# Router work between the parts of the last output products, and logits in column halves

## The reference

```python
x = x + xattn(layernorm(x), ctx)      # 16 heads of 64: q, k, v, softmax(q k / 8) v, then w_o and b_o
x = x + ffn(layernorm(x))

# ffn, tokens flat: N = 4096, E = 8 experts
logits = x_flat @ router_w + router_b
gates = softmax(logits)
_, topk_idx = top_k(gates, 2)
expert_mask = one_hot(topk_idx, 8).sum(1)
pos = cumsum(expert_mask, axis=0) - 1              # place in the expert's buffer, over all tokens
expert_mask = expert_mask * (pos < 640)            # 640 = capacity
buf = zeros(8, 641, 256).at[e_idx, pos_c].add(dispatched)[:, :640]
h = gelu(buf @ w1 + b1)                            # 8 experts, hidden 1024
out = h @ w2 + b2
y = sum over experts of gathered out * (gates * valid)
```

## Time and profile before

| | us |
|---|---|
| median of 3 runs | 1019.17 |
| lowest, highest | 1018.17, 1020.28 |
| the profiled execution | 1018.17 |
| its span, first to last instruction | 1016.3 |
| TensorE busy | 979.9 (96%) |
| VectorE busy | 769.2 (76%) |
| ScalarE busy | 624.3 (61%) |
| GpSimd busy | 284.2 (28%) |

### The profile page before, as it was taken

One profiled execution on the slowest core, in us unless ns is written; L12 is line 12 of the kernel. 1 busy time (PEld: TensorE's weight loads), 2 busy tenths in 40 slices (PEclk: granted clock), 3 DMA queues, 4 the chain that ended last, 5 costly groups with the idle time before them and its releaser, 6 DMA issues.

```text
span 1016.3 us, 23196 instructions
## 1 busy us (share of the span) xinstructions
PE 979.9 (96%) x8382; PEld 883.9 (87%) x8382; DVE 769.2 (76%) x2088; ACT 624.3 (61%) x1736; POOL 284.2 (28%) x440
## 2 busy tenths in 40 slices
PE   7889999999999999999999999999888999999996
PEld 6778888888888888888888888888678999999996
DVE  6897768878787888878787887878755666776662
ACT  5777767777776777777676777777514333344330
POOL 5542021314223131313223131311442333222233
PEclk9999999999999999999999999999999999999998
DMA  8440101101010101101010110001105543444522
GB/s 241 144 114 2 33 2 33 43 13 55 14 40 15 33 13 33 44 2 43 12 32 6 33 35 6 17 5 50 58 18 178 137 96 80 113 128 129 136 26 26
DMA packets 48431, 56.74 MB, mean 56 GB/s; under 512 B 5324, under 2 KB 44218, under 8 KB 48192
## 3 DMA queue, kind: packets, MB, share of 16 engines
q1 hardware_dynamic: 39488, 46.30, 14.7%
q0 software_dynamic: 8832, 8.98, 5.5%
HBM read 36.01 MB, written 24.20 MB: 59 GB/s over the span
## 4 chain that ended last, share of the span: by engine, by line
PE 71%; DVE 18%; ACT 5%; issue 4%; DMA 0%; POOLq 0%; POOL 0%; another core or an unknown queue 0%; ACTq 0%
PE psum L561 29%; PE psum L756 11%; PE psum L658 8%; PE psum L644 7%; PE psum L628 7%; PE psum L672 7%; DVE prob L985 5%; ACT prob L819 3%; DVE negmax L974 3%; DVE kl L922 1%; DVE al L922 1%; PE psum L566 1%; DVE stats L929 1%; PE psum L719 1%; DVE ql L963 1%
## 5 line engine op out<-in xcount | busy, mean ns | idle before, releaser
L819 ACT ACTIVATE prob<-psum,negmax 128x256 f32<-128x256 f32 x512 | 239.1, 484 | 81.6 <-DVE negmax L974 81.6
L771 ACT ACTIVATE probt<-psum 128x512 f32<-128x512 f32 x256 | 157.6, 617 | 53.4 <-PE psum L644 51.1
L974 DVE TENSOR_REDUCE negmax<-psum 128x2 f32<-128x512 f32 x256 | 160.0, 683 | 22.0 <-PE psum L628 21.9
L985 DVE TENSOR_SCALAR prob<-prob,invtot 128x256 f32<-128x256 f32 x512 | 168.0, 392 | 4.5
L644 PE MATMUL psum<-ident,prob 128*128 128x128 f32 x1024 | 154.4, 275 | 3.3 <-DVE prob L985 1.7
L644 PEld LDWEIGHTS psum<-ident,prob 128*128 128x128 f32 x1024 | 120.5, 142 | 14.5 <-issue 4.4
L898 ACT ACTIVATE hid<-psum,b1t 128x640 f32<-128x640 f32 x64 | 50.9, 795 | 133.2 <-PE psum L561 133.2
L658 PE MATMUL psum<-probt,v 128*64 128x256 f32 x1024 | 124.6, 385 | 0.8 <-ACT probt L771 0.8
L541 POOL DMA_INDIRECT out_rows<-y,rowi x40 | 65.7, 1644 | 174.5 <-DVE y L1137 169.6
L505 POOL DMA_INDIRECT slot_table<-row,picki x64 | 64.7, 1011 | 170.2 <-DVE picki L1087 143.2
L819 ACT ACTIVATION_READ_ACCUMULATOR prob<-psum,negmax 128x1 f32 x512 | 111.2, 217 | 0.0
(11 more groups left out here) (159 smaller groups left out, 2738.4 us busy)
## 6 DMA issues: line engine op xcount, KB each, us to landing
w1r<-in_w SPq DMA_DIRECT2D x8, 1024.0 KB, 8.1
w2r<-in_w SPq DMA_DIRECT2D x8, 1024.0 KB, 10.4
slot_table<-blank SPq DMA_DIRECT2D x8, 662.5 KB, 9.8
rows<-slot_table SPq DMA_DIRECT2D x7, 662.5 KB, 5.4
xin<-in_x SPq DMA_DIRECT2D x16, 256.0 KB, 3.0
out_rows<-x SPq DMA_DIRECT2D x16, 256.0 KB, 3.2
c<-in_ctxt SPq DMA_DIRECT2D x16, 128.0 KB, 3.1
c<-in_ctxt SPq DMA_DIRECT2D x32, 64.0 KB, 2.9
```

Source lines behind the costliest of these rows:

```text
L771: copy = lambda dst, src, **kw: act.activation(dst, src, ACT.Copy, **kw)
L819: last = act.activation(prob[:, m % 2, u, qb, :], psum[:, u, qb * S:(qb + 1) * S], ACT.Exp, bias=negmax[:, m % 2, u, qb:qb + 1], accum_out ...
L974: dve.tensor_reduce(negmax[:, m % 2, u, :], psum[:, u, :].rearrange("p (q s) -> p q s", q=ST), AX.X, ALU.max, negate=True).then_inc(sem("m ...
L985: last = dve.tensor_scalar(prob[:, m % 2, u, qb, :], prob[:, m % 2, u, qb, :], invtot[:, m % 2, u, qb:qb + 1], None, ALU.mult)
```

## The change

In the loop, `logits` of batch b - 2 moves from the end of a batch's fourth period to right behind its attention product, and `bias` from the next batch's first period to there. The logits are made in two halves of 64 output rows, 16 matmuls instead of 8. In the last two periods `gate`, `rank` and `pos` of batch 13 move into period 63, ahead of the last period's transposes on TensorE; the output products of batch 15 are made in two parts: 18 matmuls (`o_most`) around the last attention product, 6 behind it; the router steps of batch 14 come between; the remainders w1l move from GpSimd to VectorE (`w_rest`). Four works of batches 14 and 15 get score banks of their own (`APART`).

The diff, cut to its core:

```diff
@@ timeline(), the loop @@
         out += steps(pv, m - 2) if m >= 2 else []
+        if r == 3 and 2 <= b:
+            out += [("logits", b - 2)]
         if 3 <= b:
-            out += {0: [("bias", b - 3)], 2: [("slot", b - 3)]}.get(r, [])
+            out += {2: [("slot", b - 3)]}.get(r, [])
+        if r == 3 and 2 <= b:
+            out += [("bias", b - 2)]
...
-        if r == 3 and 2 <= b:
-            out += [("logits", b - 2)]
         out += steps("turn3 copy3", m - 1)
@@ periods 62 and 63 @@
-            *steps("exp3 v", m), *steps("logits bias shift", c), *steps(half[1], m), *steps("turn2 copy2", m - 1),
-            ("v_sb", m), *steps("o", ST * d), *steps("gate_exp gate", c), ("w_hi", 0), ("w_hi", 1),
-            ("x2add", ST * d), ("rank", c), *steps("turn3 copy3", m - 1)]
+            *steps("exp3 v", m), *steps(half[1], m), *steps("turn2 copy2", m - 1),
+            ("v_sb", m), ("o", ST * d), *steps("pick scatter", c - 1), ("w_hi", 0), ("w_hi", 1),
+            ("x2add", ST * d), *steps("turn3 copy3", m - 1)]
     m += 1
...
+    out += [*steps("scores max0 max1 exp0 exp1 max2 max3", m), *steps("pv a_hi", m - 2), ("logits", c),
+            *steps("turn0 copy0", m - 1), ("exp2", m), ("a_lo", m - 2), *steps("turn1 copy1", m - 1), ("bias", c),
+            ("exp3", m), ("shift", c), *steps(half[0], m), *steps("turn2 copy2", m - 1), *steps("turn3 copy3", m - 1),
+            ("gate_exp", c), *steps("v v_sb", m), *steps(half[1], m), *steps("gate rank", c), ("o", ST * d + 1),
+            ("pos", c), *steps("turn0 copy0", m), *steps("turn1 copy1", m), ("slot", c), ("x2add", ST * d + 1),
+            *steps("ln2_stats ln2_root", d), *steps(pv, m - 1), *steps("turn2 copy2", m), *steps("turn3 copy3", m),
+            ("o_most", ST * e), *steps("keys pick scatter", c), ("w_rest", 0), ("ln2", d), *steps("pv a_hi", m),
+            *steps("x2t x2t_sb", d), ("a_lo", m), ("o_most", ST * e + 1), ("w_rest", 1), ("logits", d),
+            ("w_hi", 2), ("w_hi", 3), ("bias", d), ("o", ST * e), ("shift", d), ("o", ST * e + 1), ("gate_exp", d),
+            ("x2add", ST * e), ("x2add", ST * e + 1), *steps("ln2_stats ln2_root", e), *steps("gate rank", d),
+            ("pos", d), ("warm", 14), ("ln2", e), *steps("slot", d), *steps("x2t x2t_sb", e), *steps("keys pick scatter", d),
+            ("logits", e), ("warm", 18), *steps("bias shift gate_exp", e),
+            *steps("gate rank pos slot keys pick scatter", e), ("w_lo", 2), ("w_lo", 3), ("warm", 90)]
@@ banks @@
+APART = {("x2t", B - 2): 2, ("logits", B - 2): 3, ("x2t", B - 1): 0, ("logits", B - 1): 1}
@@ bank() on TensorE @@
+                if (stage, n) in APART:
+                    pe.wait_ge(sem("exp"), UNITS * PERIODS)
+                    pe.wait_ge(sem("probt"), UNITS * PERIODS - 1)
+                    return psum[:, APART[stage, n], :]
@@ o() on TensorE @@
-            def o(n):
+            def o(n, chunks=range(PAIRS)):
...
+            def o_most(n):
+                o(n, range(PAIRS - 2))
+
+            def o_(n):
+                o(n, range(PAIRS - 2, PAIRS) if n >= ST * (B - 1) else range(PAIRS))
@@ logits() on TensorE @@
                 for t in range(ST):
-                    mm = products(dst[:, t * NE:(t + 1) * NE],
-                                  [(x2t[:, k, t * P:(t + 1) * P], rwt[:, k, :]) for k in range(DC)])
+                    for k in range(DC):
+                        for h in range(2):
+                            r = slice(h * HD, (h + 1) * HD)
+                            mm = pe.matmul(dst[r, t * NE:(t + 1) * NE], x2t[:, k, t * P + h * HD:t * P + (h + 1) * HD],
+                                           rwt[:, k, :], start=(k == 0), stop=(k == DC - 1))
@@ VectorE @@
+            steps = dict(..., w_rest=lambda piece: split_w(0, piece), ...)
```

More of the change, by code:

```diff
@@ L156 @@
 TURN_BANK = (4, 0, 1, 4)
-WORKS = [(s, n) for s, n in TIMELINE if s in ("xt", "q", "k", "v", "pv", "o", "x2t", "logits", "pos")]
+APART = {("x2t", B - 2): 2, ("logits", B - 2): 3, ("x2t", B - 1): 0, ("logits", B - 1): 1}
+WORKS = [(s.removesuffix("_most"), n) for s, n in TIMELINE
+         if s in ("xt", "q", "k", "v", "pv", "o_most", "x2t", "logits", "pos")
+         or s == "o" and n < ST * (B - 1)]
+WORKS = [w for w in WORKS if w not in APART]
 WORK_READ = {"xt": "xt_lo", "q": "q_lo", "k": "k_lo", "v": "v_sb", "pv": "a_lo", "o": "x2", "x2t": "x2t_sb",
@@ L660, in pv @@
                 mm.then_inc(sem("pv"), 1)
-            def o(n):
+            def o(n, chunks=range(PAIRS)):
                 b, t = divmod(n, ST)
-                dst, tt = bank("o", n), slice(t * P, (t + 1) * P)
-                pe.wait_ge(sem("a_lo"), PER_B * (b + 1) - 1)
+                dst = bank("o", n) if chunks[0] == 0 else psum[:, 5 + work["o", n] % WORK_BANKS, :]
+                tt = slice(t * P, (t + 1) * P)
+                if chunks[0] == 0:
+                    pe.wait_ge(sem("a_lo"), PER_B * (b + 1) - 1)
                 if n == 0:
                     pe.wait_ge(sem("vsplit"), 4)
-                for c in range(PAIRS):
+                for c in chunks:
                     if c == PAIRS - 2:
@@ L673, in o @@
                                        stop=(c == PAIRS - 1 and j == 2))
-                mm.then_inc(sem("o"), 1)
+                if chunks[-1] == PAIRS - 1:
+                    mm.then_inc(sem("o"), 1)
+            def o_most(n):
+                o(n, range(PAIRS - 2))
+            def o_(n):
+                o(n, range(PAIRS - 2, PAIRS) if n >= ST * (B - 1) else range(PAIRS))
             def x2t_(b):
@@ L701, in _ @@
             pe.wait_ge(sem("ident"), 1)
-            steps = dict(warm=warm, xt=xt, q=q, k=k, v=v_, scores=scores, pv=pv, o=o, x2t=x2t_, logits=logits, pos=pos,
+            steps = dict(warm=warm, xt=xt, q=q, k=k, v=v_, scores=scores, pv=pv, o=o_, o_most=o_most, x2t=x2t_, logits=logits, pos=pos,
                          turn0=lambda m: turn(m, 0), turn1=lambda m: turn(m, 1), turn2=lambda m: turn(m, 2),
@@ L1093, in split_w @@
                         w_piece((w1h, w2h)[part][r], cut)).then_inc(sem("wsplit_lo"), 1)
-            steps = dict(split_lo=split, ln1=ln1, xt_lo=xt, q_lo=q, k_lo=k, max0=lambda m: maxima(m, 0), max1=lambda m: maxima(m, 1),
+            steps = dict(split_lo=split, ln1=ln1, xt_lo=xt, w_rest=lambda piece: split_w(0, piece), q_lo=q, k_lo=k, max0=lambda m: maxima(m, 0), max1=lambda m: maxima(m, 1),
                          max2=lambda m: maxima(m, 2), max3=lambda m: maxima(m, 3), a_lo=pv, x2add=o,
```

## The result

The changed kernel takes 1024.12 us (median of 7 runs, 1022.01 to 1025.81), the kernel before 1019.17 us in runs of the same set: a ratio of 1.0047, with a 95% interval of 1.0032 to 1.0062. It is slower by 5 us, where the forecast was 1010.7 us. The profiled execution has a span of 1022.0 us against 1016.3 us, 5.7 us more, so I split these 5.7 us along the trace.

What follows compares the result with a forecast made beforehand. Two close limits per batch: TensorE's own work, about 44.8 us, and a path through VectorE and ScalarE, 45.13 us. 1018.17 - 4.3 (loop) - 4.2 (tail) = 1009.7, plus 1.0 to the median: 1010.7 us; range 1005.5 to 1017.

Steps and rivals of the forecast that it cites:

- Logits in halves: Loop, TensorE: 16 half products run in pairs on column halves and take 0.55 us, where 8 whole ones took 0.79.
- That gives TensorE 0.24 us back in each of 13 batches: Loop: the shorter logits free TensorE time in each batch, 3.1 us in all.
- The held copy: Loop, ScalarE's first probt copy, held until scatters are through: it may slip in earlier, and TensorE's waits shrink; 1.2 us gained.
- Slower: Rival, chance 0.11: held copy follows the scatters in a ring (k, q, pick, scatter, copy), 0.55 us more a batch; 1021 to 1024 us.
- The tail: Last two periods up to the last scatter: 4.2 us gained, between 1.5 and 5.5.
- (a): Last period: with logits 13, w1l on GpSimd, gate and rank 13 out of the way, the maxima start 4.3 us earlier.
- (b): Last period's transposes: pos of batch 13 in front of them waits for VectorE, so only 0.7 us is left.
- (c): Last attention product starts at 732.7 instead of 734.71; VectorE's w1l halves, 1.22 us each, stay hidden, if not up to 1.2 us.
- (d): After the last attention product: the last addition starts at 739.4 instead of 742.65, 3.3 us earlier.
- (e): Batch 14's router steps and 14 warming transposes: x2t of batch 15 starts at 745.0 instead of 747.81, 2.8 us earlier.
- (f): End of routing: only four scatters follow the last pick index, so the last scatter starts at 758.2 instead of 762.46, 4.2 us earlier.
- The experts' part as a block: Expert part after the last scatter: not touched, so it moves as a block.

Runs made afterwards that it cites:

- g2: The kernel before without the scatters of batches 0 to 11, in a set without the hold: ratio 0.9978, 44.70 us a batch.
- h3: The changed kernel with the loop's order of before, halves and new tail kept, in a set without the hold: ratio 0.9965.
- e1: The kernel before with the loop part of the change alone (logits moved and in halves, bias with them): ratio 1.0034, without the hold.
- e3: The changed kernel with the loop's order of before; halves and the new last two periods kept: ratio 0.9975, without the hold.
- g3: The kernel before without the scatters of batches 0 to 11, with the loop's part of the change: ratio 1.0009, without the hold.
- f1: The kernel before with nothing but a comment changed, in a set with the hold: 1018.81 us (one run).
- f2: The changed kernel with nothing but a comment changed, in a set with the hold: ratio 1.0077.
- g1: The changed kernel with the loop's order of before, as e3, run again without the hold: ratio 0.9963.
- i1: The changed kernel once more, in a set with the hold: ratio 1.0058.
- h1: The kernel before without the scatters of batches 0 to 11, repeating g2 without the hold: 1011.05 us (one run).
- e4: The kernel before without the scatters of batches 0 to 11, in a set without the hold: ratio 0.9990.
- g4: g1 with three edits of the last two periods (pos 13 later, 30 warming transposes before pos 14, 110 instead of 90 at the end): ratio 0.9920.
- i2: The kernel before without the scatters of batches 0 to 11, with the loop's part of the change, with the hold: 1015.44 us (one run).
- h2: The kernel before without the scatters of batches 0 to 11, with the loop's part of the change, without the hold: 1015.71 us (one run).
- f4: The changed kernel with four unneeded identity transposes in the place the logits left, in a set with the hold: ratio 1.0062.

## Why the prediction was wrong

**Logits in halves.** The term itself was right: 0.52 us against 0.55, and the loads are paired. The rule that I had weighed against it, from the Trainium skill ("TensorE: Matmul & The Clock Gate", section on packing small matmuls), does not hold in this case: by it, and the page's load figure, I had estimated 0.85 us for the 16.

**"That gives TensorE 0.24 us back in each of 13 batches": the step that failed.** I took the logits' time from one sum and put it in another, as if the old place would give back all of it. It does not, as three rows show for each order. The start of the third transposes, the logits, and the next scores; g2 (whole products), h3 (halves):

```profile
584.49 0.60 PE L648 MATMUL psum<-ident,prob 128*128 128x128 f32 x4
584.92 0.96 PE L565 MATMUL psum<-rwt,x2t 128*128 128x8 f32 x8
...
586.30 0.39 PE L632 MATMUL psum<-kh,qh 64*128 64x256 f32 x2
```

```profile
583.27 0.60 PE L653 MATMUL psum<-ident,prob 128*128 128x128 f32 x4
583.80 0.64 PE L711 MATMUL psum<-rwt,x2t 128*64 128x8 f32 x16
...
584.96 0.39 PE L637 MATMUL psum<-kh,qh 64*128 64x256 f32 x2
```

Transposes to scores: 1.81 us with whole logits between, 1.69 with halves, and in the changed kernel, with none, 593.06 - 591.46 = 1.60, because the scores need the bank that ScalarE's copy of these transposes reads. The old place gives back 0.21 us, or 0.09 of the halves' time; the new one takes 0.41 (attention product to queries' product: 1.88 us without logits in h3, 2.29 with them). The net is 0.32 us for the move of halves, where e1 less e3 says 0.33. Left in place, the halves gain 0.12 us. I had asked of the new place what the logits would wait for, and never of the old one what they hid. It was not in my rivals either.

**The held copy, 1.2 us gained: wrong in sign.** The rival *Slower* had half of the mechanism: in most batches the hold went with the scatters, and the 0.3 us waits stayed. Its price came out near the result, 1021 to 1024 us against 1024.12, but partly by luck. Up to period 62 the move costs 2.9 us with no scatter (g3 less g2), and 4.2 us in the first comparison, so the hold adds 1.3 us there. In the set of f1 and f2 it is 709.35 - 702.73 = 6.6 us, and the hold adds 3.7. The two executions of the changed kernel differ in how many copies came early: four of twelve at less than 5.0 us behind the scatter in the first, none in f2 but that of the first batch that scatters. The rival had 6 us from the ring alone. I had also thought that only the keys' copy would be left under the hold; the queries' copy is met by it too. My reason against the rival, a margin of 0.4 us, was worked out from ends of steps that were all to come 0.24 us earlier, that is from the first failed step.

**The tail, 4.2 us gained: 0.6 measured, 3.0 between g1 and g2, without the hold.** Measured from period 62's scores, which take the loop out. From there to the load of the rows it is 62.35 and 62.42 us with the hold in the kernel before (before, f1), and 61.73, 62.18 and 62.21 in the changed one (after, f2, i1): 0.1 to 0.7 us gained. Without the hold the old tail takes 61.6 to 62.4 us (e1, h1, e4, g2), the new one 59.4, 59.4 and 60.2 (e3, g1, h3): 1.4 to 3.0 us gained. g1 stands for the new tail below. It may be set against the kernel before: g2, the old tail without the hold, has the last period's transposes, the last addition and the last scatter 24.9, 40.5 and 60.3 us behind the scores, as the kernel before.
- (a) maxima 4.3 us earlier: 719.94 against 720.06 with the loop 4.21 later. Right. The rank steps at 0.3 us: right.
- (b) transposes of the last period 0.7 us earlier: they stand 26.01 us behind period 62's scores against 24.85, 1.2 us later. In g1 they are at 24.05, 0.8 us earlier. So the working was right and what came on top was the hold behind batch 12's scatters, which the change moves into period 62. I had named the hold in the tail, behind scatters 13 and 14, not behind 12.
- (c) VectorE's w1l at 1.22 us a piece: as counted, hidden.
- (d) last addition 3.3 us earlier: 0.7 with the hold (745.78 + 0.38, against 742.65), 2.7 in g1.
- (e) batch 15's transposes 2.8 us earlier: 1.2 us later with the hold, and only 0.8 earlier in g1. `pos` 14 came where I had it, 3.9 us behind the addition. The 14 warming transposes after it were sized at 0.11 us; behind 4 us of idle time they ran at the lower clock and took 753.23 - 750.08 = 3.15 us with the position products. g4, which warms in front of `pos`, starts the transposes 0.9 us behind it.
- (f) last scatter 4.2 us earlier: 0.6 with the hold, 3.0 in g1.

**The experts' part as a block: wrong by 2.1 us**, by the clock behind the load of the rows. g1 and h3 show that one kernel falls on either side, so part of this can be chance of one execution. With the hold, all three profiles of the changed kernel (after, f2, i1) have the lower clock there, and neither of the two of the kernel before (before, f1). Without it the old tail has been seen on either side (g2 and e1 with it, h1 without). Whether the change makes it likelier is open.

Of the signs that I had named, "a batch over 45.2 us" came, and "the first copy of probt less than 5 us after the first scatter" came in the first batch that scatters and in four of the other eleven.

## What to carry to other kernels

Before a piece of work is moved on a full engine, ask of its old place what it hides: look at the next instruction behind it, whose bank it needs, and who frees that bank. If the time between the neighbours can't fall below a copy on another engine, the move gives next to nothing back there (0.09 us of 0.41 here) and costs its full length in the new place. A small step that nobody waits for is the right filler for such a place, as f4 showed with work of no use at all. And a stretch in which TensorE idles can be paid for twice, as a wait and as the clock behind it.

## What the runs showed of the hardware

- While indirect scatters were issued, in some sets of runs, ScalarE started late on what it takes over from TensorE: 2.25 us behind transposes that it follows within 0.70 us otherwise, in most batches 5.7 us behind the first scatter and in some 5.0. The kernel before took about 5 us more than its 1013 to 1014 in these sets, and without the scatters of twelve batches nothing of that was left: the loop's part of the change took 1015.44 us in such a set (i2) and 1015.71 in another (h2). The same chip showed it in one set and not in another. Its cause is open, and so is whether TensorE's end, its signal or ScalarE is late.
- Column halves of 64 with a moving side of eight columns run in pairs: 16 in 0.52 us, where eight of 128 columns took 0.79 us.
- In the kernel after, four microseconds without work on TensorE (one busy microsecond of five) were followed by some 7 us at the lower clock, and 14 transposes took 3 us in it. In g1 the same 3.99 us of idle time were followed by 7 us with a mean of 0.76.
